# First attention: VectorE's additions cut in halves and put behind the second maxima of a double step

## The reference

```
xn = layer_norm(x, g1, b1)
ln_lat = layer_norm(latents, g2, b2)
q = ln_lat @ Wq
kv = jnp.concatenate([xn, ln_lat], axis=1) @ Wkv
...
weight = jnp.where(full_mask[:, None, None, :], weight, neg)
weight = jax.nn.softmax(weight.astype(jnp.float32), axis=-1).astype(q.dtype)
out = jnp.einsum('bhln,bhnd->bhld', weight, v)
...
return out @ Wout
```

## Time and profile before

| | |
|---|---|
| median of 3 runs | 3269.82 us (3268.73 to 3271.04) |
| the profiled execution | 3268.37 us, its span 3266.5 us |
| first attention's 32 units | from 93.7 us (first exponentials) to 2294.6 us (start of the last `add_up`) |
| PE, DVE, ACT, POOL busy in the span | 2956.8, 2435.5, 1801.1, 2101.2 us |
| one group of four units, steady | 277.4 us |

### The profile page before, as it was taken

How to read it: one execution, slowest core, us unless ns; L and a number is a source line. 1 busy time by engine, 2 the same in 40 slices (tenths; PEclk the granted TensorE clock), 3 DMA queues, 4 the chain that set the end, 5 groups by cost and what they waited for, 6 DMA issues and landing times. The chain is left out here.

```text
span 3266.5 us, 53578 instructions
## 1 busy us (share of the span) xinstructions
PE 2956.8 (91%) x21712; PEld 1094.2 (33%) x21720; DVE 2435.5 (75%) x3023; ACT 1801.1 (55%) x2009; POOL 2101.2 (64%) x1000
## 2 busy tenths in 40 slices
PE   5899999999999999999999999998597799999977
PEld 3233333333333333333333333322454133333334
DVE  8777787677777778767777776782545888888878
ACT  4455555455445555555554555445433488888863
POOL 5787988898898888889879888989510111111022
PEclk9999999999999999999999999999698799999989
DMA  1000000000000000000000000000210100000000
GB/s 62 6 1 1 1 8 1 1 7 1 1 7 1 1 1 7 1 1 7 1 1 1 2 1 1 1 1 1 68 32 14 43 8 7 6 7 8 5 3 25
DMA packets 24615, 28.72 MB, mean 9 GB/s; under 512 B 6511, under 2 KB 21296, under 8 KB 24370
## 3 DMA queue, kind: packets, MB, share of 16 engines
q1 hardware_dynamic: 24370, 25.31, 2.6%
HBM read 17.42 MB, written 2.10 MB: 6 GB/s over the span
## 5 line engine op out<-in xcount | busy, mean ns | idle before, releaser
L348 POOL TENSOR_TENSOR a_acc<-a_acc,a_prob 128x1024 f32<-128x1024 f32 x704 | 1725.3, 2451 | 297.7 <-ACT a_prob L480 216.0
L598 DVE TENSOR_REDUCE a_part_max<-wide 128x2 f32<-128x1024 f32 x880 | 1069.1, 1215 | 443.1 <-PE wide L885 442.3
L480 ACT ACTIVATE a_prob<-slot,a_mask_bias 128x1024 f32<-128x1024 f32 x928 | 986.9, 1113 | 738.6 <-PE slot L914 721.7
L929 PE MATMUL bank<-a_prob,a_val 128*64 128x512 f32 x3712 | 897.1, 605 | 2.1 <-ACT a_prob L480 2.1
L1218 ACT ACTIVATE a_prob<-slot,a_mask_bias 128x1024 f32<-128x1024 f32 x416 | 455.2, 1115 | 67.0 <-PE slot L1418 53.9
L885 PE MATMUL wide<-a_k_hi,a_q_hi 64*128 64x512 f16 (+1 forms) x2016 | 352.4, 362 | 113.8 <-DVE a_part_max L598 106.0
L1262 DVE TENSOR_REDUCE a_part_max<-wide 128x1 f32<-128x512 f32 x514 | 333.5, 684 | 37.6 <-PE wide L1406 20.8
L929 PEld LDWEIGHTS bank<-a_prob,a_val 128*64 128x64 f32 x3712 | 226.5, 136 | 394.0 <-issue 289.4
L914 PE MATMUL slot<-a_q_hi,a_k_lo 64*128 64x512 f16 x1856 | 352.4, 376 | 0.0
L914 PE MATMUL slot<-a_q_hi,a_k_step_hi 64*128 64x512 f16 x1728 | 327.9, 376 | 2.4 <-ACT a_prob L480 2.3
L914 PE MATMUL slot<-a_q_lo,a_k_step_hi 64*128 64x512 f16 x1728 | 327.7, 376 | 0.0
(11 more groups left out here) (397 smaller groups left out, 3274.7 us busy)
## 6 DMA issues: line engine op xcount, KB each, us to landing
a_w_staged<-in_w SPq DMA_DIRECT2D x8, 384.0 KB, 3.2
x_res<-in_x SPq DMA_DIRECT2D x4, 512.0 KB, 5.8
a_q_op<-a_hi SPq DMA_DIRECT2D x128, 16.0 KB, 1.8
out_x<-x_res SPq DMA_DIRECT2D x16, 128.0 KB, 1.7
a_k_op<-mid_k_hi SPq DMA_DIRECT2D x32, 52.0 KB, 2.2
mid_context<-in_ctxt SPq DMA_DIRECT2D x1, 1601.0 KB, 6.7
mid_w_staged<-in_w1a SPq DMA_DIRECT2D x4, 384.5 KB, 6.5
a_acc<-in_ctx SPq DMA_DIRECT2D x3, 512.0 KB, 8.4
```

The source lines that it names most:

```text
L348: nc.gpsimd.tensor_tensor(acc, before, prob[:, k % R, :], ALU.add).then_inc(added_p, 1)
L480: nc.scalar.activation(prob[:, k % R, :], m.slot[k % 2][:, :], ACT.Exp, bias=mbias[:, t:t + 1]).then_inc(probs_ready, 1)
L598: nc.vector.reduce_max(part_max[:, w % 2, :, j, c], pairs, AX.X).then_inc(max_used, 1)
L929: ins = nc.tensor.matmul(av[r, :], val[g % 2][:, t, r], prob[:, k % R, h * QB:(h + 1) * QB], start=(t == 0), stop=(t == NT - 1), tile_posi ...
```

## The change

Nothing is computed differently; the order on VectorE changes, and who adds which tile.

```
-        self.sums_at, self.invert_at, self.pieces, self.divide_at, self.out_at = 9, 12, 4, 16, (17, 19)
-        self.last_pair, self.turn_at = 24, 25
-        self.dve_tiles = [5, 7, 9, 15, 17]
+        self.sums_at, self.invert_at, self.divide_at, self.out_at = 9, (11, 13, 15, 17), 17, (19, 21)
+        self.pieces = len(self.invert_at)
+        self.last_pair, self.turn_at, self.shift_at = 24, 25, 27
+        self.dve_tiles = [0, 1, 5, 17, 21]
+        self.add_at = {3: (1, 0), 5: (1, 1), 7: (2, 0), 9: (2, 1), 19: (3, 0), 21: (3, 1), 23: (4, 0), 25: (4, 1)}
...
-        adds_v, adds_p = len(a.dve_tiles) - 1, len(a.pool_tiles) - 1
+        adds_v, adds_p = 2 * (len(a.dve_tiles) - 1), len(a.pool_tiles) - 1
...
-                nc.vector.tensor_tensor(acc, before, prob[:, k % R, :], ALU.add).then_inc(added_v, 1)
+                nc.vector.tensor_tensor(acc, before, prob[:, k % R, c], ALU.add).then_inc(added_v, 1)
...
-                    if t == a.turn_at and w + 1 < a.units:
+                    if t == a.shift_at and w + 1 < a.units:
                         shift_of(w + 1)
-                    if w and 0 <= t - a.invert_at < a.pieces:
-                        invert(w - 1, t - a.invert_at)
+                    if w and t in a.invert_at:
+                        invert(w - 1, a.invert_at.index(t))
...
-                    if t - 2 in a.dve_tiles:
-                        add(w, t - 2)
-                    elif w and t + NT - 2 in a.dve_tiles:
-                        add(w - 1, t + NT - 2)
-                    if k - 3 in a.job_at and a.job_at[k - 3][1] < a.nkq:
-                        step_low(*a.job_at[k - 3])
+                    if t in a.add_at:
+                        add(w, *a.add_at[t])
+                    ago = 3 if t < 3 else 4
+                    if t % 2 and k - ago in a.job_at and a.job_at[k - ago][1] < a.nkq:
+                        step_low(*a.job_at[k - ago])
```

More of the change, by code:

```diff
@@ L478, in weigh @@
                     else:
-                        act.wait_ge(added_v, adds_v * v + max(a.dve_tiles.index(s), 1))
+                        act.wait_ge(added_v, adds_v * v + 2 * max(a.dve_tiles.index(s), 1))
                 nc.scalar.activation(prob[:, k % R, :], m.slot[k % 2][:, :], ACT.Exp, bias=mbias[:, t:t + 1]).then_inc(probs_ready, 1)
@@ L615, in shift_of, with add @@
                 nc.vector.tensor_tensor(shift[w % 2][:, :, :], rows, mine, ALU.mult).then_inc(shift_ready, 1)
[L617 to L621, removed]
+            def add(w, n, half):
+                k = w * NT + a.dve_tiles[n]
+                c = slice(half * QB, (half + 1) * QB)
+                if n == 1 and half == 0 and w >= 2:
                     dve.wait_ge(total_ready, w - 1)
                 dve.wait_ge(probs_ready, k + 1)
-                acc = acc_v[:, w % 2, :]
+                acc = acc_v[:, w % 2, c]
                 before = acc
-                if n == 0:
-                    before = prob[:, (w * NT + a.dve_tiles[0]) % R, :]
-                else:
-                    dve.wait_ge(added_v, adds_v * w + n)
-                nc.vector.tensor_tensor(acc, before, prob[:, k % R, :], ALU.add).then_inc(added_v, 1)
+                if n == 1:
+                    before = prob[:, (w * NT + a.dve_tiles[0]) % R, c]
+                else:
+                    dve.wait_ge(added_v, adds_v * w + 2 * (n - 2) + half + 1)
+                nc.vector.tensor_tensor(acc, before, prob[:, k % R, c], ALU.add).then_inc(added_v, 1)
             def invert(w, piece):
@@ L776, in _ @@
                             residual(w - 1, z)
-                    if t - 2 in a.dve_tiles:
-                        add(w, t - 2)
-                    elif w and t + NT - 2 in a.dve_tiles:
-                        add(w - 1, t + NT - 2)
-                    if k - 3 in a.job_at and a.job_at[k - 3][1] < a.nkq:
-                        step_low(*a.job_at[k - 3])
-            for t in range(NT, NT + 2):
-                if t - 2 in a.dve_tiles:
-                    add(a.units - 1, t - 2)
+                    if t in a.add_at:
[3 more added lines that the diff above has]
+                        step_low(*a.job_at[k - ago])
             for piece in range(a.pieces):
```

## The result

| | before | after |
|---|---|---|
| median of 4 runs each | 3270.43 us (3268.73 to 3271.58) | 3314.66 us (3313.96 to 3315.29) |
| profiled execution, its span | 3268.37, 3266.5 us | 3315.29, 3313.4 us |
| DVE, POOL busy | 2435.5, 2101.2 us | 2651.9, 2093.0 us |
| steady group, its units u = 0 to 3 | 277.4: 67.8, 69.5, 70.0, 70.1 | 284.2: 69.6, 69.1, 76.0, 69.4 |

The ratio is 1.0134, with a 95% interval of 1.0119 to 1.0148: slower by 44 us. A unit's length here is the distance between its first exponentials and those of the next.

What follows compares the result with a forecast made beforehand. TensorE was taken to set the pace, with only its waits for VectorE's maxima to win. 3268.4 + 30 (waits) + 0 (last group) + 4 (clock) = 3302, against the median 3304 us; range 3280 to 3325.

Steps and rivals of the forecast that it cites:

- rival 4: Worse: clock falls in each u = 2 and halves set GpSimd back until ScalarE waits for `prob`; 3312 to 3330, 15%.
- What bounds: Steady group: TensorE, busy 263.9 of 277.4 us, sets the pace; only its waits can be won, 9.8 us a group.
- What an addition costs: VectorE's additions: a half ends 0.55 us behind GpSimd's current addition or takes 0.68 alone; that wait is paid eight times a unit.
- Rival 1: Faster: halves on VectorE cost half the mean, 1.14 us each; 4.3 us a group won, 3236 us, 7%.
- Unit u = 2: Late maxima behind double steps 4, 6, 8 and 10: 6.6 us together; all waits of this unit 8.5 us.
- Rival 3: VectorE keeps the port for `step_low` directly behind its half: double step 6 late by 0.9 us; 3278 to 3295 us, 25%.
- Rival 2: Waits by luck of phase: if GpSimd's tiles 4, 9, 11 begin 0.3 us later, time within 0.2%; 5%.
- double step 10: In u = 2, the 128-column `step_low` ends behind GpSimd's tile 11, making the next maxima late by 1.9 us.
- The sum of the waits: TensorE's waits for maxima over four units: 16.8 us against 12.5, so +4.3 a group, +30 in seven.
- Halves at 19, 21, 23: Halves on VectorE standing before outputs or a job: 0.1 to 0.2 us in all.
- The clock: TensorE's falls to 1.2 GHz from long waits in u = 2: 1.7 us each, 4 us taken, ends 0 and 12.
- The last group: The group without jobs, after the seven: between -2 and +4 us, taken as 0.

Runs made afterwards that it cites:

- low_first: The changed kernel with `step_low` ahead of the half addition in the odd step: 3314.25 us, ratio 1.0143.
- low_odd_alone: The kernel before with only `step_low` moved to the odd step, four steps behind its job, additions whole: 3327.55 us, ratio 1.0180.
- low_even: The changed kernel with `step_low` back in the even step, between the two maxima: 3273.0 us, ratio 1.0012.
- whole_low_even: `low_even` with VectorE's four additions whole again, at steps 3, 7, 19 and 23: 3251.52 us, ratio 0.9946.

## Why the prediction was right, and where it was off

The prediction was 3304, in a range of 3280 to 3325, with slower at 85%; 3314.66 was measured. The likeliest case, 3295 to 3312, was missed by 2.7 us: the time lies in that of rival 4, the worse one. Of its mechanism one half came true, the fall of the clock in each u = 2; the other, ScalarE waiting for GpSimd, did not: between 96 and 2275 us no such wait for an addition of GpSimd is listed, where before had 14.0 us.

**What bounds.** Right. TensorE set the pace before and sets it after, and all that changed are its waits for the maxima and its clock.

**What an addition costs.** Right. Of the 256 halves of the changed kernel, 225 stood beside an addition of GpSimd, and each of these ended 0.545 to 0.554 us behind its end; all 256 take 1.82 us in the mean (465.7 us in all, 289.2 before for 128 whole ones). The Trainium skill's rule (SBUF — State Buffer, section "SBUF: two separate sides"), that the shared pair of ports is locked for a whole instruction, agrees with all of these ends, and with the 7.2 us that are left without GpSimd's additions. Of the other 31 halves 25 lasted 0.68, and 6 ended 0.55 behind another operation of GpSimd. Rival 1, a shared rate with halves of 1.14 us, falls with it.

**Unit u = 2.** Right in its largest number. Foretold and measured: behind double step 4 0.76 and 0.78; behind 6 3.1 and 3.15; behind 8 0.8 and none; behind 10 1.9 and 0.38; the division 0.4 and 0.64; the half at 25 0.7 and 0.72. Rival 3, that VectorE keeps the port for `step_low` behind its half, is refuted by the 2.83 us at 1389.80, by `low_first`, and by `low_odd_alone`, which it would have made cheaper. Rival 2, luck of phase, fell where it counted most: tile 4 of GpSimd began 0.24 us ahead of the half and was served first. At double step 10 the phase did turn out in the change's favour (below). These two rows show tile 4, of DVE and then of POOL:

```profile
1381.90 2.67 DVE L631 TENSOR_TENSOR a_acc<-a_prob 128x512 f32<-128x512 f32 x1
```

```profile
1381.66 2.36 POOL L350 TENSOR_TENSOR a_acc<-a_acc,a_prob 128x1024 f32<-128x1024 f32 x1 [1.92 <-ACT a_prob L482]
```

**The sum of the waits.** The term of 4.3 us a group was a little small: 5.2 to 5.3 in six groups and 3.3 in the first, in seven 34.7 and not 30. By units, forecast and measured: u = 0 4.0 and 5.9, u = 1 2.3 and 2.5, u = 2 8.5 and 7.3, u = 3 2.0 and 2.0. The total came near in part by luck: in u = 2 too much was foretold, in u = 0 too little. Four sizes were off:

- "Halves at 19, 21, 23 stand before outputs or a job: 0.1 to 0.2 in all." In u = 2 the two behind steps 19 and 21 cost 0.62 + 0.32, in u = 0 0.48 + 0.32. The half at 19 lasted 2.79 us (it began just behind a tile of GpSimd and waited for all of it), against a room of 1.05 and 1.06 more for TensorE's outputs. I had priced the wait of these halves near its middle. The residual then stands between the next maxima and carries the lateness on.
- In u = 0 double step 4 cost 1.08 and not 0.75, double step 8 with the half at step 9 0.49 and not 0.1, `step_low` at step 11 1.11 and not 0.9.
- Reciprocal and division together cost 0.64 and not 0.4, in every unit, so 1.0 a group. I had let the division overlap the reciprocal by 0.15; it starts 0.10 behind its end (0.96 from 1413.93, then 1414.99), and the next maxima 1.66 behind the reciprocal's start instead of 1.47.
- "Double step 10 ... late by 1.9" was 0.38. By my times the 128 columns would meet GpSimd's tile 11 just begun. They started at 1402.72, when tile 10 was about to end (it had begun at 1400.84, 1.6 us later than I had it), and lasted 0.62:

```profile
1402.72 0.62 DVE L589 TENSOR_TENSOR a_k_lo<-a_k_step,a_k_step_hi 128x128 f16<-128x128 f32 x1
```

That is the weak point which the prediction named: three double steps on, GpSimd's phase, worked out to 0.2 us, had drifted by 1.6 us, and the clock had a part in it.

**The clock.** The mis-sized term that matters. I took 4 us between ends of 0 and 12. The records show one fall to 0.50 in each of the seven units u = 2, and each goes with the wait of 3.1 us: three begin 0.4 to 1.2 us behind its end, four 0.5 to 1.1 us before it, while TensorE still stands (at 257.6, 540.9, 824.2, 1107.5, 1394.2, 1677.5 and 1960.8 us; those at 1107.5 and 1960.8 last 6.83 us, the others 3.41). PE's timeline right behind the wait at 1393.83, values that take 1.94 us at the full clock:

```profile
1394.15 3.63 PE L926 MATMUL bank<-a_prob,a_val 128*64 128x512 f32 x8
```

The seven units u = 2 together grew by 43.8 us and their waits by 31.0; the 12.8 left over are the slower clock's. All other units of the seven groups grew by 3.8 and their waits by 3.7. So the clock cost 13 us, a little over my upper end of 12. It also took the place of a wait: double step 8 shows none, where 0.8 was foretold, and TensorE itself was late there. That the falls come from the long wait is supported by `low_even`, which has neither, by `low_first` (seven waits of 3.1 to 3.2 us, seven falls) and by `low_odd_alone`, whose 14 waits of 3.6 us and more, in u = 0 too, went with 14 falls. `whole_low_even` has a wait of 1.67 in each of seven groups and no fall. Nothing was tried that kept the one without the other.

**The rest.** ScalarE did wait for halves of VectorE, eight times and 19.4 us in all, where I had said that they were ahead of the exponentials; no wait of TensorE's values came of it: in the whole program they waited 0.2 us for exponentials. The last group, taken as 0, came out at -1.5: its first three units took 63.3, 63.7 and 61.2 us against 62.5, 65.3 and 61.9, and the fall of the clock of before did not come again. `shift_of` went without idle time and is a gain of 6.5 us by itself. The sum by measured terms is 34.7 + 12.9 - 1.5 = 46, the first exponentials come 1.3 later, and the spans differ by 46.9. Of the forecast's error, the waits are 5 and the clock 9; the last group takes 1.5 back, and 2 more go the same way, because the profiled execution of before lay 1.4 under its median and that of after 0.6 over.

**What the prediction did not ask.** It took the change as one whole. Taken apart, from the changed kernel down: `step_low` some 41 us; of the 3 to 4 us that `low_even` then still has over the kernel before, halving is +21.5, the division and the outputs about +5, `shift_of` -6.5, which leaves about -16 for the new tiles and steps of the additions. This last number is a difference that no run measured by itself; it supposes that the parts add up (`shift_of` was moved in the kernel before), and may be off by 5. So the gain seems to have been there, in the places of the additions; halving gave it back, and the place of `step_low` cost the rest.

## What to carry to other kernels

Where two engines exclude each other for whole instructions, price an instruction by the rest of the other engine's running one and then its own work, and count how many such instructions there are: cutting one in two halves only its own work and pays the wait twice. Don't put two of them one behind the other on the engine that others wait for: here a queued one of the other engine got in between, whichever of the two stood first. And read a moved instruction against the room at its new place in microseconds, in the worst phase too: behind the second maxima there was more room than between them, and `step_low` needed 2.8 us of it instead of 0.68.

## What the runs showed of the hardware

- The port changes hands between two instructions of VectorE that follow each other without a pause, if GpSimd has one queued (1389.80: 2.83 us for 0.68 of work). The row of `low_odd_alone` at 1123.01 is the extreme: 128 columns in 2.43 us.
- A single wait of TensorE of 3.1 us went with a fall of its clock to 1.2 GHz in seven units of seven, of 3.41 or 6.83 us, begun between 1.1 us before the wait's end and 1.2 behind it. I had expected this of some of them only. Waits of 1.9 us in the last group went with one sometimes: in the kernel before that at 2124.91 did, that at 2190.5 did not.
- GpSimd's additions, which run beside TensorE and are 86% of a group's time, cost the kernel before 87 us of 3270. 71 of these are `pair`'s waits for maxima (101.6 less 30.9, from 96 to 2275 us). The program's time behind the stage's last exponential is 15.5 us longer with them (985.7 against 970.2).
